# Attention and switch layer in one program, with the router's early rows prepared in the attention's last units

## What is computed

```python
x = x + tanh(g_xattn[0]) * window_attention(layernorm(x), ctx, ctx)     # 16 heads of 16, window 128
x = x + tanh(g_ffn[0])   * switch(layernorm(x))                         # 16 experts, top 1, 128 places each
x = x + tanh(g_xattn[1]) * linear_attention(layernorm(x), ctx, ctx)
x = x + tanh(g_ffn[1])   * top2(layernorm(x))                           # 8 experts, top 2

def switch(xf):                        # xf: 2048 x 256
    score = softmax(xf @ Wg + bg)      # 16 logits for each token
    gate, idx = max(score), argmax(score)
    pos = place of the token in its expert's list, in token order; keep = pos < 128
    y = relu(xf_of_expert @ W1[e] + b1[e]) @ W2[e] + b2[e]
    return where(keep, y * gate, 0)
```

## Time and profile before

| | us |
|---|---|
| median of 3 runs (lowest, highest) | 809.45 (809.12, 810.59) |
| the profiled execution, whole | 819.22 |
| its span, first to last instruction | 817.5 |
| mean granted clock of PE | 0.952 of full |
| PE busy | 728.4 (89%) |
| PEld, DVE, ACT, POOL busy | 605.5, 373.0, 320.4, 338.4 |

### The profile page before, as it was taken

One profiled execution on the slowest core, in us unless ns is written; L12 is line 12 of the kernel. 1 busy time (PEld: TensorE's weight loads), 2 busy tenths in 40 slices (PEclk: granted clock), 3 DMA queues, 4 the chain that ended last, 5 costly groups with the idle time before them and its releaser, 6 DMA issues. The chain is left out here.

```text
span 817.5 us, 16602 instructions
## 1 busy us (share of the span) xinstructions
PE 728.4 (89%) x5335; PEld 605.5 (74%) x5335; DVE 373.0 (46%) x1091; ACT 320.4 (39%) x860; POOL 338.4 (41%) x453
## 2 busy tenths in 40 slices
PE   5878999898798999996889885699999999999994
PEld 2446666675575999995766653599999999999994
DVE  3477777776326754442877868111222211222111
ACT  4336676666404333330456530133332233322231
POOL 5133333332206555443246521535544455544332
PEclk9989999999859999997999987999999999999998
DMA  5966666555493799923244544436653443354311
GB/s 143 215 139 125 122 125 124 118 118 143 139 374 119 246 375 358 340 89 116 30 61 70 118 133 156 133 93 164 199 137 68 106 109 60 53 148 119 85 23 14
DMA packets 146834, 114.61 MB, mean 140 GB/s; under 512 B 50465, under 2 KB 138188, under 8 KB 146762
## 3 DMA queue, kind: packets, MB, share of 16 engines
q1 hardware_dynamic: 136490, 100.59, 45.5%
q0 software_dynamic: 10272, 13.13, 7.7%
HBM read 153.02 MB, written 24.40 MB: 217 GB/s over the span
## 5 line engine op out<-in xcount | busy, mean ns | idle before, releaser
L1021 ACT ACTIVATE e_hT<-e_HP,e_col 128x128 f32<-128x128 f32 x312 | 89.1, 369 | 190.0 <-PE e_HP L985 176.3
L985 PEld LDWEIGHTS e_HP<-e_rT,w_up 128*128 128x128 f32 x1248 | 145.4, 192 | 2.1 <-DVE e_rT L1033 0.2
L985 PE MATMUL e_HP<-e_rT,w_up 128*128 128x128 f32 x1248 | 145.9, 275 | 0.6 <-issue 0.6
L997 PE MATMUL e_Y<-w_down,e_hT 128*128 128x256 f32 x624 | 142.4, 382 | 2.1 <-issue 2.1
L997 PEld LDWEIGHTS e_Y<-w_down,e_hT 128*128 128x128 f32 x624 | 116.6, 192 | 16.7 <-issue 2.2
L1043 DVE TENSOR_TENSOR e_yo<-e_Y,e_b2b 128x256 f32<-128x256 f32 x39 | 16.6, 425 | 223.0 <-PE e_Y L997 223.0
L1078 POOL DMA_INDIRECT out<-e_yo,d_table x39 | 63.1, 1619 | 129.8 <-DVE e_yo L1046 115.0
L423 DVE TENSOR_REDUCE a_nm<-S 128x2 f32<-128x512 f32 x128 | 83.5, 684 | 40.7 <-PE S L490 40.4
L327 ACT ACTIVATE a_pexp<-S 128x1024 f32<-128x1024 f32 x64 | 64.7, 1016 | 31.5 <-PE S L508 31.2
L808 PEld LDWEIGHTS e_HP<-e_rT,w_up 128*128 128x128 f32 x512 | 59.5, 192 | 3.3 <-issue 1.8
L808 PE MATMUL e_HP<-e_rT,w_up 128*128 128x128 f32 x512 | 60.0, 275 | 2.1 <-issue 1.6
(11 more groups left out here) (328 smaller groups left out, 1240.0 us busy)
## 6 DMA issues: line engine op xcount, KB each, us to landing
w_up<-L_ffn_w_in SPq DMA_DIRECT2D x39, 1024.0 KB
w_down<-L_ffn_w_in SPq DMA_DIRECT2D x39, 1024.0 KB
w_up<-L_ffn_W_in SPq DMA_DIRECT2D x16, 1024.0 KB
w_down<-L_ffn_W_in SPq DMA_DIRECT2D x16, 1024.0 KB, 9.0
e_b2b<-L_ffn_b_in SPq DMA_DIRECT2D x55, 128.0 KB
scr<-a_parts SPq DMA_DIRECT2D x51, 128.0 KB
a_q<-scr SPq DMA_DIRECT2D x17, 192.0 KB
a_k<-scr SPq DMA_DIRECT2D x17, 192.0 KB
```

The lines of the kernel that those rows point to most:

```text
L985: i = e.matmul(HP[r][:, j, :], w1[:, n % WR, k, P * j:P * j + P], rT[:, r, k, :], start=(k == 0), stop=(k == 1))
L997: i = e.matmul(Y[r][:, 0:D], hT[:, r, j, :], w2[:, n % WR, j, :], start=(j == 0), stop=(j == NJ - 1))
L1021: i = e.activation(hT[:, r, j, :], HP[r][:, j, :], ACT.Gelu, bias=col[:, n % 4, j:j + 1])
```

## The change

1. Attention and switch layer become one block: `attention` returns its five streams (`Head`), and the switch layer's streams begin with them. The barrier between them is gone.
2. `RowNorm` replaces `layer_norm_rows`. DVE takes the variances of groups 0 to 2 at the end of steps 13 to 15, POOL the roots after its steps 14 to 16, and DVE (before, ACT) normalises 12 row tiles at the end of steps 15 and 16, then tiles 12 and 13 after the last unit; ACT does tiles 14 and 15. The hardware loop has two turns, so that steps 11 on are written out.
3. `Router`: PE turns the row tiles, two at a time, in steps 16 and 17 (pairs 0 to 5), into the score banks of pass 1 that are free then; DVE and ACT copy them; the logits lie in bank `M`. Pairs 0 and 1 are multiplied by Wg in step 17, 2 to 5 after the last unit, 6 and 7 last. The filler products between are gone. Normalised and turned rows lie in the buffers of the expert weights `w1`.
4. SP stores three groups of rows, loads `w2` of experts 0 and 1, stores the last group, waits until that has landed and all rows are turned, and loads the rest of the weights of experts 0 to 3. `lin.unstage` moves behind the last logits.
5. `mark_places`: the places' one-hot matrix is built by 16 tensor_scalar instructions from a bf16 row instead of one tensor_tensor, with a signal after every fourth, and `list_products` waits for each quarter. `list_table` makes the fetch column first, and POOL fetches rows before the store column is there (`stored`).
6. In the top-2 layer: `mark_places` twice, `spos` ahead of `rhs`, `rhs` from a contiguous row `slots`, and 10 filler products ahead of the counts, not 20.

```diff
-LOOP_FROM, LOOPS = 3, 3
+LOOP_FROM, LOOPS = 3, 2
+MEASURE_AT, ROOT_AT = {13: 0, 14: 1, 15: 2}, {14: 0, 15: 1, 16: 2}
+EARLY = 3 * GT
@@ attention, DVE's step
+                if n.reg is None and n.c == NU + 1:
+                    route.keep_turned_vector(e, 1)
...
-                if n.reg is None and 15 <= n.c <= 17:
-                    e.wait_ge(s_xw, 4 * (n.c - 3))
-                    next_dve(e, n.c - 15, n.c - 15)
+                if n.reg is None and n.c == NU - 1:
+                    rows_ln.shift(e, 0)
+                    route.normalise(e, 0, GT)
+                if n.reg is None and n.c in MEASURE_AT:
+                    g = MEASURE_AT[n.c]
+                    e.wait_ge(s_xw, 4 * 4 * (g + 1))
+                    rows_ln.variances(e, g)
+                if n.reg is None and n.c == NU:
+                    route.keep_turned_vector(e, 0)
+                    rows_ln.shift(e, 1)
+                    route.normalise(e, GT, 2 * GT)
+                    rows_ln.shift(e, 2)
+                    route.normalise(e, 2 * GT, EARLY)
+                if n.reg is None and n.c == NU + 1:
+                    route.keep_turned_vector(e, 2)
+                    route.keep_turned_vector(e, 3)
             over_units(e, step)
             e.wait_ge(s_xw, 4 * NU)
-            next_dve(e, 3, 3)
+            rows_ln.variances(e, 3)
+            rows_ln.shift(e, 3)
@@ attention, PE
+            def router(step, u):
+                if step == 0 and u == 1:
+                    e.wait_ge(s_mx, HU * NU)
+                    route.turn(e, 0)
+                if step == 0 and u == 3:
+                    route.turn(e, 1)
+                if step == 1:
+                    route.turn(e, 2 + u)
+                if step == 1 and u == 2:
+                    e.wait_ge(s_mte, NU)
+                    route.multiply(e, 0)
+                if step == 1 and u == 3:
+                    route.multiply(e, 1)
@@ class Router
+    def normalise(self, e, first, end):
+        e.wait_ge(self.norm.s_nm, first // GT + 1)
+        for t in range(first, end):
+            e.tensor_scalar(self.xn[:, t, :], self.K["x"][:, t, :], self.norm.rstd[:, t:t + 1], self.norm.nmr[:, t:t + 1],
+                            ALU.mult, ALU.add).then_inc(self.s_ln, 1)
+    def turn(self, e, u):
+        if 2 * u + 2 <= LATE:
+            e.wait_ge(self.s_ln, 2 * u + 2)
+        else:
+            e.wait_ge(self.s_la, 2 * u + 2 - LATE)
+        if u >= 2:
+            self.copied(e, u - 2)
+        for t in range(2):
+            for k in range(2):
+                i = e.transpose(self.T[u % 2][:, t, k, :], self.xn[:, 2 * u + t, P * k:P * k + P], self.K["identf"][:])
+        i.then_inc(self.s_t, 1)
@@ switch_layer
             def route_sync(e):
...
+                before.sync(e)
+                store_rows(e, K["rows"], route.xn, s_sc, range(3), ready)
+                load(0, 1)
+                load(1, 1)
+                store_rows(e, K["rows"], route.xn, s_sc, (3,), ready)
+                e.wait_ge(route.s_t, NT // 2)
+                e.wait_ge(s_sc, 16 * (NT // GT))
+                load(0, 0)
+                load(1, 0)
+                e.wait_ge(route.s_l, NT // 2)
+                load(2, 0)
+                e.wait_ge(lin.s_kc, 2)
+                load(2, 1)
+                load(3, 0)
+                load(3, 1)
             def route_tensor(e):
...
+                before.tensor(e)
+                lin.turn(e, IN_START, turned)
+                route.multiply(e, 2)
+                route.multiply(e, 3)
+                lin.multiply(e, IN_START, products)
+                route.multiply(e, 4)
+                route.multiply(e, 5)
+                route.turn(e, 6)
+                route.turn(e, 7)
+                route.multiply(e, 6)
+                route.multiply(e, 7)
@@ lists
+def mark_places(e, oh_pos, pos, place, s):
+    for t in range(NT):
+        i = e.tensor_scalar(oh_pos[:, t, :], place, pos[:, t:t + 1], None, ALU.is_equal)
+        if t % 4 == 3:
+            i.then_inc(s, 1)
@@ top2_layer
-                keep_clock(e, C, K, 20)
+                keep_clock(e, C, K, 10)
```

More of the change, by code:

```diff
@@ L173, in step @@
                     lin.load(e)
+                if n.reg is None and n.c == 13:
+                    route.load(e, a)
                 m = n - 1
@@ L293, in step @@
                     rsqrt(STATISTICS_AT[n.c])
+                if n.reg is None and n.c in ROOT_AT:
+                    rows_ln.root(e, ROOT_AT[n.c])
             over_units(e, step, -2, NU)
@@ L338, in step @@
                     exps(m, 0)
+                if n.reg is None and n.c == NU + 2:
+                    route.keep_turned_scalar(e, 4)
                 if (m - 1).valid():
@@ L896, in _ @@
                     fetch(n)
+                head.stored(e)
                 for n in range(tiles + 1):
@@ L1130, in list_scaled, with list_products @@
                         ALU.mult).then_inc(s, 1)
-def list_products(e, lists, oh_pos, rhs, first, last):
+def list_products(e, lists, oh_pos, rhs, first, last, s, marked):
     for t in range(NT):
+        if t % 4 == 0:
+            e.wait_ge(s, marked + t // 4 + 1)
         i = e.matmul(lists, oh_pos[:, t, :], rhs[:, t].rearrange("p a n -> p (a n)"), start=(first and t == 0),
```

356 lines of the change are left out of this document (165 added, 191 removed).

## The result

| | us |
|---|---|
| changed kernel, median of 20 runs (lowest, highest) | 808.70 (802.15, 814.01) |
| kernel before, 20 runs on the same chip | 813.84 (808.11, 820.49) |
| ratio, 95% interval | 0.9941 (0.9916 to 0.9966) |
| the profiled execution, whole | 809.44 |

Against the same chip's runs of the kernel before the change gains 0.6%, some 5 us, where 22 were forecast; 808.7 lies outside the range 778 to 799. A second measurement, beside later experiments, gave 805.47 and 0.9956 (0.9927 to 0.9986). The three runs of the kernel before that the prediction had (809.12 to 810.59) are the first of the 20 here, and lie low among them: the 20 have their median at 813.84, and three of them took 818.56 to 820.49, like the profiled 819.22.

What follows compares the result with a forecast made beforehand. PE was taken to bound nearly everywhere, at half its clock behind the attention. Terms -23.5 + 0 + 6.7 - 5.0 = -21.8 us took the profiled 819.2 to 797.4, carried to the median as 787.6; range 778 to 799.

Steps and rivals of the forecast that it cites:

- A: From the attention's last add to the logits on DVE: 7.0 us instead of 30.5, -23.5 (bounds -22 and -24.5).
- D: The last layer's top-2 routing, from fillers to turned rows: -5.0 us (-7.5 to -1.5).
- B: From the logits to the first expert product of the switch layer, now 18.8 us: 0 (-2.8 to +3.5).
- C: The attention's last units, which take in the early variances, normalisations, turns and logit steps: +6.7 us (+3 to +10).
- rival 1: Early work in in-order streams delays the attention's units 14 and 15 more than forecast: 793 to 800, chance 0.14.
- The loop's -0.5: In the attention, one turn of the hardware loop less: -0.5 us (0 to -1).
- The fillers' -1.6: Last layer's routing: ten filler products fewer let the counts start earlier, -1.6 us (-0.8 to -2.3).
- The -0.9 for the position: Last layer's routing: spos moved ahead of POOL's work, -0.9 us (0 to -0.9).
- Rival 3: In the routing, marks are slow (798) or POOL and DVE hold each other up (791): chance 0.08.
- Rival 2: PE's clock stays full behind the attention, with no barrier and fewer narrow products: 778 to 783, chance 0.12.
- Rival 5: Switch experts run at the pace of their weights, since `w1` loads late: slower, 821 at 220 GB/s, chance 0.05.
- Rival 4: Early rows don't help, the last four tiles' path being as long as all sixteen's: 805 to 810, chance 0.03.

Runs made afterwards that it cites:

- e5_before_again: The kernel before, nothing edited, for another profiled execution: 807.2 us, ratio to itself 0.9963; the profiled execution took 806.65.
- e9_all: Changed kernel with router parameter loads earlier, early normalisations behind norm on DVE, POOL's copy earlier, weights of experts 2 and 3 later: 795.92 us, ratio 0.9843.
- e7_switch_start: Changed kernel with POOL's copy of staged values ahead of the logits and weights of experts 2 and 3 behind the first fetched rows: 800.21 us, ratio 0.9901.
- e12_two_turns: Kernel before with two turns of the attention's hardware loop instead of three: 808.17 us, ratio 0.9982.
- e13_loads_and_start: Changed kernel with early parameter loads, POOL's copy earlier and weights of experts 2 and 3 later, DVE's order as in the change: 801.03 us, ratio 0.9894.
- e2_router_late: Changed kernel with the 12 early normalisations, six early turns, their copies and first two logit steps moved behind the last unit: 818.14 us, ratio 1.0101.
- e6_after_again: The changed kernel once more, nothing edited: 805.47 us, ratio 0.9956 to the kernel before.
- e11_turns_late: `e9_all` with the six early turns, their copies and first two logit steps behind the last unit, normalisations early: 807.09 us, ratio 0.9982.
- e4_top2_only: Kernel before with only the change's top-2 routing (marks, slots, filler count, table order): 807.13 us, ratio 0.9986.

## Why the prediction was wrong

**The step that failed first** is the one that carried the sum over: "The median of the runs, 809.45, lies 9.8 under the profiled execution; the same step gives 787.6." That holds only if the 9.8 us lie outside of what the change removes. Against `e5_before_again` (span 12.5 us shorter) most of them lie inside: 10.3 in A's stretch and 2.1 in D's, with 4.2 in the top-2 experts, and against these 2.1 in B's stretch, 1.5 to the last add and 0.5 between. I had the signs before me, a clock of 0.50 in the earlier trace rows and an execution 8.6 us over the slowest of the three runs shown, and took the half clock of that stretch for its price. The median of three that I carried to was itself 4.4 us under the median of all 20 runs.

**A.** The mechanism was right: no barrier, only four tiles' work left. But an ordinary execution has 20.2 us there, so the change gives 9 to 12 and not 23.5. The end, forecast at 7.0 us behind the last add, was 8.6 and 10.9: I counted four products to a logit step where the rows have eight, so two steps took 2.82 and 3.44 us, not 1.7; at full clock they take 1.96 and the stage 7.7 (`e9_all`).

**B.** ±0 was right for its time (20.1 and 21.0 against 20.6 to 21.0), but two terms in it were too small. POOL's copy beside DVE's chain, "+0.4 (0 to +1.5)", cost 1.9: the step of line 755 stood still for the rest of the copy. I had written down what the Trainium skill, SBUF — State Buffer, section "SBUF: two separate sides", would make of it (+1.5) and gave it the smaller weight. The traces agree with that rule: 2.29 us beside the copy, 0.42 without. The fetch beside weight loads, "+0.5 (0 to +2)", was a wait of 3.0 and 1.0 us. But an ordinary execution of the kernel before waits for it too, as PE's list of waits in `e5_before_again` shows:

```profile
PE e_T L797 <- DMA e_rows<-rows,b_table: 3.2, 1, 3.2
```

Only where the narrow run took 10 us longer had the weights landed by then; so the base of 18.8 was 2 us short, as A's was 10 too long.

**C** is mis-sized: "C = +6.7 (+3 to +10)". From unit 15's preparation on, the changed kernel's two executions take 53.9 and 54.3 us, and `e7_switch_start` with the same attention 50.1, where three ordinary ones of the kernel before take 43.1 to 43.4: +7 to +11. Unit 15 to 16 is 1.3 longer; I had 1.2 for variances behind unit 13, but `e12_two_turns`, without variances there, is 0.6 longer too, so up to half of it may be the unrolled step. Behind unit 15 four normalisations and the variances stand in front of norm, and PE waits 3.5 us for it, where I had 1.8: this is rival 1's mechanism, and its "there are no maxima left" did not help, since PE's product needs norm at once. The order alone is worth 4.1 (`e13_loads_and_start` against `e9_all`), of which some 3.4 may be the clock by the estimate under the table: 6.8 us at half clock against none. Unit 15's loads wait for SyncE, where three parameter loads are issued ahead of its hand-over in step 13, and PE waits 2.4, 2.1 and 1.2 for them. Neither this queue nor a clock that falls around the attention's waits had a term in my sum. Turns, copies and logit steps are 4.1 (+2.0 forecast). The loop's -0.5 was nothing.

**D** is mis-sized: -5.0 was -2.4 against the profile the prediction used and -0.3 to -0.8 against `e5_before_again`. The fillers' -1.6 was a property of the half clock (7.05 us for 20 then, 4.3 for 19 at full clock). "So 0.15" for a mark was nearly right, 0.163; what made 7.3 us of the 4.8 is that the first two marks are 1.0 us longer each, beside POOL's two products. The -0.9 for the position was real on its own row (0.19 against 1.12), but that hold-up went over to the marks. The Trainium skill, VectorE: DVE Perf Modes, section on the TRN2 errata, made 194 ns of a mark at 1 element a cycle and 94 ns at 4, estimates I put beside the sum; the trace agrees with neither, by the 163 ns between marks that nothing holds up. The list products ran at half clock in the changed kernel, 2.43 against 1.76. rhs and the table came as forecast.

**The rivals.** Rival 1's mechanism came true in C, short of its "+12 or more", and its 793 to 800 failed with the carried-over 9.8. Rival 3's small version came true in its mechanism and near its sizes (1.9 us beside the copy where it had 1.5, 2.0 in the marks where it had 0.9 in each list), and its 791 failed likewise. Rival 2 did not come: the clock fell in the attention and again behind it. Rival 5 did not: no kernel here waits for weights in the switch experts. Rival 4 is refuted by `e2_router_late` (1.0101) against `e6_after_again` (0.9956), and again by `e11_turns_late` (807.09) against `e9_all` (795.92): the early rows save 11 to 12 us. Of my signs of being wrong, the last add past 218 came (221.4 and 219.8), and two marks took over 0.3 us; PE waited for no weight. And "0.2% from no change" was too fine: with 20 runs a side the interval is still 0.25% to each side.

Summed with what the runs showed, against an ordinary execution: A -9 to -12, B -1 to 0, C +7 to +11, D -1 to 0, so -7 to +2. The two measurements say -4.8 and -3.6, inside that; the kernel against itself said -3.0. That the change gains anything is therefore likely, and not shown beyond doubt.

## What to carry to other kernels

Before a gain is read off one profile, set that execution's own time and granted clock beside the runs: if it is slow, find the stretch in which it is, and price that stretch at both clock levels. Work moved ahead into another stage's in-order streams costs what waits behind each instruction, its DMA issues too, and a wait of PE can cost more than its length, as the clock may fall with it; here another order on DVE, earlier parameter loads, a moved copy and later weight loads turned half a per cent into 1.6%. And a POOL copy of 2.35 us belongs where DVE is idle: beside it a step of 0.42 us took 2.29.

## What the runs showed that I had not expected

- PE's clock over the same stretch of the same instructions is 0.50 in one execution (30.5 us) and 0.89 in three others (20.2, 20.3, 19.9). Where the turns were moved behind the attention it was 0.50 both times (30.0 and 24.5 us). In the fast ones the clock had fallen and come back in PE's gap, before the narrow work (`e5_before_again`, `e12_two_turns`), or did not fall until behind it (`e4_top2_only`, 1.00 from 204 to 228 us). What sets the place stays open, as no run was made to tell it.
- The clock from 43 to 75 us varies between 0.71 and 0.89 too, and what lies behind moves with it: unit 15 was prepared at 165.5 to 171.0 us.
- POOL's product of 256 columns took 0.65 us beside DVE's marks, one of which was 0.4 us longer for it, and 2.72 beside its big compare. The difference, 2.07 us, is that between one compare and one mark (2.29 and 0.24).
- From the issue of the first indirect fetch of 128 rows to their turn it is 3.2 us with the later weight loads held back, and 6.4 and 4.4 beside them. The wait of PE that follows is 3.0 and 1.0 us.
- The kernel before, measured against itself, gave 0.9963 with an interval that leaves out 1.
